# Self-attention's entry and exit in a fused perceiver layer: who rounds the weights, in which order two engines split them and normalise, and which bank takes the last two dense groups

## The reference

```python
x = x + xattn(layernorm(x), ctx, mask, Wq, Wk, Wv, Wo)   # 16 heads of 128, 8 key heads, 2048 keys
x = x + attn(layernorm(x), w_q, w_kv, w_dense)           # 16 heads of 128 in 4 groups, causal, 128 keys
x = x + ffn(layernorm(x), gate, bias, shared, experts)   # 16 experts, top 2, F = 128
# attn:
q = x @ w_q; k, v = split(x @ w_kv)
probs = softmax(where(causal, q @ k.T * SCALE, -inf))
out = (probs @ v).reshape(b, s, 16 * 128) @ w_dense
```

## Time and profile before

| | us |
|---|---|
| median of 3 runs (lowest, highest) | 375.74 (375.56, 376.29) |
| the profiled execution, its own time | 377.27 |
| its span on the core | 375.5 |
| PE busy | 343.1 (91%) |
| DVE, POOL, ACT busy | 286.7, 244.6, 226.5 |
| cross-attention's steady groups | about 50 to 231 |
| self-attention's entry, groups, exit | about 250 to 279, to 314, to 332 |
| experts | about 332 to the end |

### The profile page before, as it was taken

How to read it: one execution, slowest core, us unless ns; L and a number is a source line. 1 busy time by engine, 2 the same in 40 slices (tenths; PEclk the granted TensorE clock), 3 DMA queues, 4 the chain that set the end, 5 groups by cost and what they waited for, 6 DMA issues and landing times.

```text
span 375.5 us, 6913 instructions
## 1 busy us (share of the span) xinstructions
PE 343.1 (91%) x2240; PEld 308.1 (82%) x2240; DVE 286.7 (76%) x481; ACT 226.5 (60%) x402; POOL 244.6 (65%) x150
## 2 busy tenths in 40 slices
PE   4886689998999999999999998996989999898996
PEld 1765578997997997997998887996988897698995
DVE  3489968987987987987987977535457745769997
ACT  2468487677686685685685677642035455246772
POOL 4917499699679579579669579464234843746550
PEclk9999999999999999999999999997599999969999
DMA  7504885877777777778668668842016011133640
GB/s 214 201 2 112 203 202 131 214 177 169 179 171 168 183 166 174 183 160 180 155 147 182 161 145 210 220 138 84 2 33 192 0 57 58 28 101 106 178 134 29
DMA packets 33332, 52.07 MB, mean 139 GB/s; under 512 B 5792, under 2 KB 23328, under 8 KB 33312
## 3 DMA queue, kind: packets, MB, share of 16 engines
q1 hardware_dynamic: 33168, 51.56, 54.9%
q10 hardware_dynamic: 144, 0.26, 0.4%
HBM read 20.08 MB, written 0.26 MB: 54 GB/s over the span
## 4 chain that ended last, share of the span: by engine, by line
PE 74%; DVE 12%; issue 5%; SPq 2%; DMA 2%; ACT 2%; POOL 2%; DVEq 0%; ACTq 0%
PE bank L536 12%; PE bank L537 11%; PE bank L538 11%; PE pair L536 10%; PE pair L538 10%; PE pair L537 10%; SPq L261 2%; PE bank L776 2%; DVE probs L1304 2%; DVE blocks L1315 1%; DVE xn L1242 1%; PE pair L732 1%; DMA resid<-in_x_dram 1%; PE pair L768 1%; PE pair L762 1%
## 5 line engine op out<-in xcount | busy, mean ns | idle before, releaser
L408 POOL TENSOR_TENSOR pT<-pT,pT_hi 128x1024 fp32r<-128x1024 f32 x60 | 142.6, 2406 | 40.7 <-ACT pT_hi L1013 40.5
L1003 ACT ACTIVATE probs<-probs,lowest 128x2048 f32<-128x2048 f32 x32 | 64.3, 2009 | 45.0 <-DVE lowest L1304 45.0
L536 PE MATMUL bank<-pT_hi,ctx_lo 128*128 128x256 f32 x240 | 68.2, 284 | 1.1 <-POOL pT L408 1.1
L537 PE MATMUL bank<-pT,ctx_hi 128*128 128x256 f32 x240 | 68.7, 286 | 0.0
L538 PE MATMUL bank<-pT_hi,ctx_hi 128*128 128x256 f32 x240 | 68.1, 284 | 0.0
L1013 ACT ACTIVATE pT_hi<-pT 128x1024 fp32r<-128x1024 f32 x60 | 61.5, 1050 | 10.1 <-DMA pT<-blocks 9.0
L536 PE MATMUL pair<-ctxT_hi,qk_lo 128*128 128x512 f32 x128 | 51.6, 403 | 6.2 <-DVE lowest L1304 2.3
L538 PE MATMUL pair<-ctxT_hi,qk_hi 128*128 128x512 f32 x128 | 50.1, 391 | 0.0
L537 PE MATMUL pair<-ctxT_lo,qk_hi 128*128 128x512 f32 x128 | 50.0, 391 | 0.0
L536 PEld LDWEIGHTS bank<-pT_hi,ctx_lo 128*128 128x128 f32 x240 | 45.3, 189 | 2.5 <-POOL pT L408 1.5
L537 PEld LDWEIGHTS bank<-pT,ctx_hi 128*128 128x128 f32 x240 | 45.1, 188 | 1.0
(11 more groups left out here) (230 smaller groups left out, 857.8 us busy)
## 6 DMA issues: line engine op xcount, KB each, us to landing
pT<-blocks SPq DMA_DIRECT2D x128, 128.0 KB, 2.3
pT<-ctx_raw SPq DMA_DIRECT2D x112, 128.0 KB, 2.3
ctx_raw<-ffn_experts_gate_up_dram SPq DMA_DIRECT2D x16, 256.0 KB, 3.1
wq<-in_L_xattn_Wq_dram SPq DMA_DIRECT2D x8, 256.0 KB, 2.9
wo<-in_L_xattn_Wo_dram SPq DMA_DIRECT2D x8, 256.0 KB, 3.0
blocks<-in_L_attn_w_q_dram SPq DMA_DIRECT2D x4, 512.0 KB, 4.0
blocks<-in_L_attn_w_dense_dram SPq DMA_DIRECT2D x4, 512.0 KB, 4.0
ctx_raw<-_L_ffn_experts_down_dram SPq DMA_DIRECT2D x16, 128.0 KB, 2.6
```

Of the source, the lines that this page charges most:

```text
L408: pool.tensor_tensor(dst, src, hi.bitcast(F32), ALU.subtract).then_inc(ready, 1)
L536: pe.matmul(dst, w[1], x[0], start=start, stop=False)
L537: pe.matmul(dst, w[0], x[1], start=False, stop=False)
L1003: act.activation(probs[:, j], probs[:, j], ACT.Exp, bias=lowest[:, p, j, 1:2], scale=-1.0, accum_out=den[:, p, j:j + 1]).then_inc(exps, 1)
```

## The change

- In every cross-attention group DVE makes `oT_rest` of the first sequence two places earlier, ahead of `add_out` and the denominators.
- Entry: ACT rounds all weights of group 0 (k, v and dense too) while cross-attention still runs; POOL splits q and k ahead of `power`, and waits for `xn` before it splits dense. DVE makes `oT_rest` ahead of `xnT_rest`; ACT copies `oT` and `yT` ahead of the copies of `xn`; PE moves the last `y_project` ahead of the queries, `out_project` ahead of the third head, and the second `xn_transpose` ahead of `scores2(0, 0)`. Of 8 `keep_warm` matmuls on entry 1 is left.
- Groups: the last group's dense weights go into `wq2`'s place, with a load that no longer waits for the dense group before; ACT rounds them, the four first experts and their down-projections inside the groups. POOL splits two experts ahead of the last two dense weights.
- Exit: the last two dense groups sum in `D_LAST`, so one addition to the residual goes. They are cut by sequence and woven with the transposes. `keep_warm` goes from 8 + 2 + 4 + 9 + 5 to 8 + 1 + 5 + 2 + 2. All expert splits stand ahead of the last norm's `power`, and DVE rounds nothing there.

```diff
@@ SP
+                if isinstance(r, int) and r == R - 1:
+                    sp.wait_ge(wq2_ready, R)
+                    dst, done = wq2, ld_wd2_last
+                else:
+                    after(sp, wd2_ready, r)
+                    dst, done = wd2, ld_wd2
@@ POOL
-            power(0, 1)
             split_q(0)
             split_k(0)
+            power(0, 1)
+            pool.wait_ge(xn_ready, B + 1)
             split_d(0)
             power(1, 1)
+            pool.wait_ge(xn_ready, 2 * B)
             split_q(1)
...
-            for r in range(R - 2, R):
-                normalise(r)
-                split_d(r)
+            normalise(R - 2)
             split_expert(0, 0)
             split_expert(0, 1)
-            for b in range(B):
-                power(b, 2)
+            split_d(R - 2)
+            split_d(R - 1)
+            normalise(R - 1)
             split_expert(0, 2)
             split_expert(0, 3)
             split_down(0)
             split_down(2)
+            for b in range(B):
+                power(b, 2)
@@ PE
+            def last_group2():
...
+                for b in range(B):
+                    scores2(R - 1, b)
+                attend2(R - 2)
+                keep_warm(QA, 8)
+                for b in range(B):
+                    dense_end(R - 2, b)
+                    turn2(R - 1, b)
+                attend2(R - 1)
+                keep_warm(QA, 1)
+                for b in range(B):
+                    dense_end(R - 1, b)
...
             xn_transpose(0, 1, WQK_BANK)
+            y_project(LAST, G - 1)
             pe.wait_ge(xnT_ready, B + 1)
             pe.wait_ge(wq2_ready, 1)
             query(0, of[0], first_q)
-            y_project(LAST, G - 1)
             query(1, of[0], first_q)
+            out_project(LAST, G - 1)
             query(2, of[0], first_q)
-            out_project(LAST, G - 1)
             query(3, of[0], first_q)
             keys_values2(0, of[0], first_kv)
-            keep_warm(bank[4], 2)
+            xn_transpose(1, 1, WQK_BANK)
+            keep_warm(bank[4], 1)
...
             scores2(0, 0)
-            keep_warm(bank[4], 1)
-            xn_transpose(1, 1, WQK_BANK)
-            keep_warm(bank[4], 5)
@@ ACT
             act.activation(wq2_hi, wq2, ACT.Copy).then_inc(wq2_hi_ready, 1)
+            act.activation(wk2_hi, wk2, ACT.Copy).then_inc(wk2_hi_ready, 1)
+            act.activation(wv2, wv2_raw, ACT.Copy).then_inc(wv2_ready, 1)
             yT_copy(LAST - 1)
+            act.activation(wd2_hi, wd2, ACT.Copy).then_inc(wd2_hi_ready, 1)
...
                 if behind:
-                    copy_qk(r + 1)
+                    copy_q(r + 1)
+                if r == 1:
+                    for s in range(RING):
+                        act.activation(gu_hi[:, s], ring_gu[:, s].rearrange("p k f -> p (k f)"),
+                                       ACT.Copy).then_inc(gu_hi_ready, 1)
+                if r == R - 2:
+                    for s in range(RING):
+                        act.activation(dn_hi[:, s], ring_dn[:, s], ACT.Copy).then_inc(dn_hi_ready, 1)
+                    act.wait_ge(qb_psum, R)
+                    act.wait_ge(ld_wd2_last, 16)
+                    act.activation(wq2_hi, wq2, ACT.Copy).then_inc(wd2_last_hi_ready, 1)
+                if behind:
+                    copy_k(r + 1)
@@ DVE
                 mask_pair(g, 4)
+                oT_rest(2 * (g - 1), O_BANK[0], 0)
                 if out_on:
                     add_out(2 * (g - 2) + 1, 2 * (g - 2) + 1, 1)
                 denominators(2 * (g - 1) + 1, 1)
                 mask_pair(g, 5)
-                oT_rest(2 * (g - 1), O_BANK[0], 0)
...
             norm_apply(0, 1)
+            oT_rest(LAST, O_BANK[0], 0)
             xnT_rest(0, 1, WQK_BANK)
-            oT_rest(LAST, O_BANK[0], 0)
-            round_kv(0)
             yT_rest(LAST)
-            round_d(0)
...
             rest_c(R - 1)
-            round_gu(0)
-            round_gu(1)
             finish_rows(0)
-            round_gu(2)
             finish_rows(1)
```

More of the change, by code:

```diff
@@ L348, in load_d @@
             def load_d(r):
-                after(sp, wd2_ready, r)
-                sp.dma_start(wd2.rearrange("p (h n) -> p h n", h=HR), sd_v[r]).then_inc(ld_wd2, 16)
+                if isinstance(r, int) and r == R - 1:
[4 more added lines that the diff above has]
+                    dst, done = wd2, ld_wd2
+                sp.dma_start(dst.rearrange("p (h n) -> p h n", h=HR), sd_v[r]).then_inc(done, 16)
             load_qkv(0)
@@ L477, in split_d @@
             def split_d(r):
-                pool.wait_ge(wd2_hi_ready, r + 1)
-                rest(wd2_lo, wd2, wd2_hi, wd2_ready)
+                if isinstance(r, int) and r == R - 1:
+                    pool.wait_ge(wd2_last_hi_ready, 1)
+                    rest(wq2_lo, wq2, wq2_hi, wd2_ready)
+                else:
+                    pool.wait_ge(wd2_hi_ready, r + 1)
+                    rest(wd2_lo, wd2, wd2_hi, wd2_ready)
             def normalise(r):
@@ L496, in _, with split_expert @@
             split_k(2)
-            with pool.Fori(1, R - 2) as r:
+            def split_expert(i, s):
+                pool.wait_ge(gu_hi_ready, RING * i + s + 1)
+                rest(gu_lo[:, s], ring_gu[:, s].rearrange("p k f -> p (k f)"), gu_hi[:, s], gu_ready)
+            for r in range(1, R - 2):
                 normalise(r)
@@ L804, in group2 @@
                     attend2(r - 1)
[L805 to L808, removed]
+                queries2(r + 1, both)
                 if before:
                     dense2(r - 1)
-                if behind:
-                    keys_values2(r + 1, both, kv2_psum)
+                keys_values2(r + 1, both, kv2_psum)
                 for b in range(B):
-                    pe.wait_ge(s2_probs, 2 * r + b + 1)
-                    for h in range(HR):
-                        mm = pe.transpose(PC[b][:, h * P:(h + 1) * P], p2[:, b, h], ident[:])
-                    mm.then_inc(p2T_psum, 1)
+                    turn2(r, b)
+            def last_group2():
+                pe.wait_ge(qa_ready, R)
+                pe.wait_ge(qb_ready, R)
+                pe.wait_ge(k2_ready, R)
+                for b in range(B):
[9 more added lines that the diff above has]
+                    dense_end(R - 1, b)
             both, of = slice(0, B * T), [slice(b * T, (b + 1) * T) for b in range(B)]
@@ L1170, in _ @@
             group2(0, False, True)
-            with act.Fori(1, R - 1) as r:
+            for r in range(1, R - 1):
                 group2(r, True, True)
@@ L1174, in _ @@
             copy_c(R - 1)
-            for s in range(RING):
-                act.wait_ge(ld_dn[s], 16)
-                act.activation(dn_hi[:, s], ring_dn[:, s], ACT.Copy).then_inc(dn_hi_ready, 1)
             def silu(m, s):
@@ L1530, in group2 @@
                     round_q(r + 2)
-                if before:
+                if before and behind:
                     add2(r - 1)
```

69 lines of the change are left out of this document (38 added, 31 removed).

## The result

The changed kernel takes 363.43 us (median of 4 runs, 361.95 to 363.58) against 376.01 for the kernel before on the same chip (4 runs): ratio 0.9648, 95% interval 0.9619 to 0.9677. The forecast was 363.4, from a range of 360.8 to 370.8. The profiled execution took 363.58, with a span of 361.8, so that the span is 13.7 us shorter than the 375.5 of before.

What follows compares the result with a forecast made beforehand. PE bounds self-attention's groups, DVE the expert loop; entry and exit stretches suffer from half clock. 1.1 + 8.5 - 0.3 + 3.0 = 12.3 us off 377.27 gives 365.0 profiled, 363.4 median; range 360.8 to 370.8.

Steps and rivals of the forecast that it cites:

- Part 1: Cross-attention loop: DVE's cycle binds, groups only 0.05 us shorter, the last group hands on its gain; 1.1 us.
- Part 2: Entry: shorter first `xn` (2.0), clock kept up and PE's new order bring the second sequence forward; 8.5 us after slips.
- I take it that it stays: Entry: PE's clock stays at full rate because idle pieces shrink to about 0.2, 0.5 and 0.1 us.
- the early fall: Rival, entry: the clock falls all the same and queries run at half clock; 370.7 us, chance 0.18.
- Part 3: Groups: the last dense load lands near 307, so ACT's copies come late; 0.3 us lost.
- Part 4: Exit: earlier residual addition and short last `xn` (2.1), faster router `bias_b` (0.6), clock (0.4), less 0.1 rounding; 3.0 us.
- the clock's 0.4: Exit: L905 takes 0.75 us less if the clock stays up; half counted because idle pieces hardly shrink.
- The 0.6: Exit: the router's `route<-route,bias_b` falls from 0.82 to 0.2 us once POOL's splits no longer run beside it.
- PE-bound: Rival, cross-attention: PE alone bounds it, so all 5.2 us of waits come back; 359.3 us, chance 0.05.
- slower: Rival, entry into groups: the clock stays low into the PE-bound stretch; 382.5 us if until 295, chance 0.04.
- no effect: Rival, whole change: `xn` stays slow or the last load lands 10 us late; about no change, chance 0.05.
- The later fall: Rival, entry: the clock falls once, in the wait for the second `xn`, 2.5 us lost; 365.9 us, chance 0.16.

Runs made afterwards that it cites:

- the loop alone: Kernel before with one edit, DVE making `oT_rest` of the first sequence two places earlier in each cross-attention group: 376.04 us, ratio 0.9981.
- the 14 matmuls: Changed kernel with 8 + 6 matmuls whose result nobody reads, in two idle stretches of PE at the start of cross-attention: 362.71 us, ratio 0.9626.
- the kernel before with PE kept busy on entry: Kernel before with 13 more `keep_warm` matmuls around the transposes of the first `xn`, nothing else: 371.03 us, ratio 0.9863.
- the entry alone: Kernel before with only the changed kernel's entry, on all four engines: 367.63 us, ratio 0.9764.
- the 1.75 that POOL's wait won: Changed kernel with one more wait: POOL splits the fifth expert only when DVE's router operations are done: 361.31 us, ratio 0.9604.

## Why the prediction came out right, point by point

**Part 1, the loop: mechanism right, 1.1 was too much.** DVE's cycle does bind: the groups went from 27.96 to 27.90 apart, the predicted 0.05, and PE's wait moved to `yT_lo`. The last group did hand on its gain: from the start of its last mask (231.94, now 232.26) to the variance (253.79, now 252.99) 1.12 us are won, against 1.14 forecast. What failed is the silence on groups 1 and 2. There `oT_hi` comes late, and an instruction moved ahead of the additions and masks makes them wait too (0.94 and 0.53). The means above say 0.4 won by the loop where 1.1 was forecast; the runs of the loop alone say 0.1 to 1.4. What those two groups cost the program is not shown: with the 14 matmuls the second of the waits (0.53) is gone as well, and leaving both groups at the old place brought no time that the runs can tell.

**Part 2, the entry: right as a sum, wrong in its split.** 2.0 for `xn`, 3.4 for the clock, 3.4 for the order became 2.5, 3.8 and 1.5, with 7.8 us in all against traces that share the old entry. The order of PE's work is the term that was mis-sized most, at more than twice what it measured. In the trace that the prediction was made from it is 9.1, because there the same old entry took 1.3 us longer than in the other two traces that have it (56.9 against 55.6), with PEclk at 0.77 from 250 to 280 against 0.83. The sentence "I take it that it stays" was right, but the chance of 0.18 for the early fall was set without seeing on what it hung. It hung on POOL's wait: with the order new and `xn` slow, the clock fell after 2.25 us of idle PE, and 6.9 us of the entry's 7.8 were lost. The Trainium skill (TensorE: Matmul & The Clock Gate, part 1) has the gate close after idling and open after sustained work. The traces agree in direction with both halves: in the run without POOL's wait the clock fell behind 2.25 us of idle PE, stayed at 0.50 while PE was busy for 10.00 of 10.00 us, and stood at 1.00 from 270.0 on.

**Part 3, the groups: 0.0 instead of -0.3.** The stretch of entry and groups is 55.66 with groups and exit changed and 55.60 with the loop alone changed. The last load was waited for until 295.82, which is 305.7 in before's times (this stretch is 9.92 earlier); I had put its landing near 307. The copy of k waited for PE behind it. The term was mis-sized by the estimate of when the second of two loads lands.

**Part 4, the exit: 2.1 + 0.6 right, the clock's 0.4 was 1.2.** The traces with the old exit tell it apart. In two of them, the loop alone and the kernel before with PE kept busy on entry, the clock did not fall on exit, and the stretch from scale to router is 21.80 us in both, against 18.92 now: 2.88, where 2.1 + 0.6 was forecast. Before's own trace has 23.01, 1.2 more, since there it fell; it fell in the entry alone too, which has 23.61. The prediction's "idle pieces there hardly shrink, so I count half" was the step that failed. In before's trace PE idles 0.44 and 1.35 us ahead of the last norm's transposes; the 1.35 goes with the slow `xn`, and in the changed kernel the longest of these is 0.56. The clock fell on exit in two of four traces of the old order and in none of the nine of the new one that keep its `keep_warm`. Not all of the 1.2 reaches the end of the span: what follows the router takes 42.33 in the loop alone and 41.80 in before.

**The 0.6 and its rule.** It came back as forecast (0.82 to 0.19), and the split put beside the router brought it back (0.83). The Trainium skill (GPSIMD Engine Reference, section 8, Key points) names two kinds of DVE instruction that contend with GpSimd, those with two SBUF inputs and those in a two-port mode. The multiplication (0.94, now 0.18) is of the first kind; the `TENSOR_SCALAR` of one input (1.29, now 0.17) would have to be of the second, but no trace shows an instruction's mode. The prediction spoke of the rule only for the exit and the dense roundings. Two such rows stood in before's trace further down the router's chain, beside POOL's splits from 337.65 to 340.42: the same `TENSOR_SCALAR` with 0.93 and the last multiplication with 1.21, together some 1.8 us too long. Neither the change nor I took them.

**The total: two errors that met.** In the traces 13.7 us were won, not 12.3. And I carried before's 1.5 us between profiled execution and median over to the changed kernel. The changed kernel's profiled execution stands only 0.15 above its median. 1.4 too little won and 1.4 too much subtracted gave 363.4; that the forecast was hit to 0.03 is luck. I take the 1.5 to be mostly clock time at entry and exit, which the change removes, but this is argued and not shown. For it: other traces of the same old entry and exit are 1.3 and 1.2 us shorter, and of the 48 runs of the kernel before that were timed beside the experiments the six with the lowest mean granted clock (0.964) took 377.3 to 378.0 us, the thirteen at 0.975 or more 375.2 to 376.5. Against it: at 0.973, the clock of the profiled execution, they took anything from 375.2 to 378.7.

**Handed on whole.** The prediction took everything won ahead of the expert loop as won at the end. Nearly, but not quite: the last stretch is 0.31 longer than in before.

**The rivals.** PE-bound and slower are excluded by the loop alone and by the clock at 1.00 in the groups; "no effect" by `xn` at 0.41 and the ratio of 0.9648. The later fall, in the wait for the second `xn`, did not come with PE idle for 0.66 there.

## What to carry to other kernels

Some DVE instructions in SBUF are held to the end of a long POOL instruction beside them (here the `TENSOR_SCALAR` that writes `xn`, 2.42 for 0.41, and a small addition, 0.83 for 0.19; a reciprocal was not held). What that costs can be more than the delay itself, when the idle PE behind it loses its clock: 2 us here became 7. So first ask which waits of PE come just ahead of dense work, and put the other engine's work elsewhere, if need be by a wait. Before more is rebuilt, a few matmuls without use in such a wait tell what the clock is worth (5.2 us here, where the whole entry was worth 8.9); and two executions should be read before the distance of a profile from its median is taken as fixed.

## What the runs showed that I had not expected

- The start of cross-attention varies by itself. Its fifth mask of group 1 starts between 56.74 and 57.89 in fourteen traces, whatever the kernel. The mean clock between 30 and 45 us sorts them: 1.00 in six (57.53 to 57.89; two of them have the 14 added matmuls), 0.89 in three (56.74 to 56.94), 0.77 in five (57.35 to 57.61). The full clock is not the earliest. Why stays open.
- An instruction held by POOL cost DVE's chain 0.63 on the router and 0.06 at the end of the span: the expert loop can take in such a delay, but took in only 0.2 of the 1.75 that POOL's wait won.
- Half clock on exit differs between traces with the same old exit (router stretch 21.80 twice, 23.01 and 23.61), although PE idles 0.44 and 1.35 ahead of the transposes in the trace of the loop alone, where it did not fall, just as in before, where it did. What decides was not tried.
